# Table numbers read four per register load in a graph attention and relation kernel

## The reference

```python
h = relu(layernorm(x))                                   # layer 0: attention with 8 heads
Q, K, V = h @ Wq, h @ Wk, h @ Wv
score = (Q[dst] * K[src]).sum(-1) / sqrt(32) + relu(edge_attr @ W1 + b1) @ W2 + b2
alpha = softmax of score over the edges of one dst
x = x + segment_sum(alpha * V[src], dst) @ Wo + bo
h = relu(layernorm(x))                                   # layer 1: 16 relations with gates
msg = (h @ W_rel[type])[src] * edge_weight * sigmoid(h @ gate_rel[type])[src]
x = x + relu(segment_sum(msg, dst))
```

## Time and profile before

| | |
|---|---|
| median of 3 runs | 5581.06 us (5578.73 to 5584.89) |
| the profiled execution, its own time | 5578.26 us |
| its span, first to last instruction | 5576.5 us |
| busy over the span | PE 86%, DVE 63%, ACT 59%, POOL 58% |
| mean granted clock of TensorE | 0.878 |

### The profile page before, as it was taken

One profiled execution on the slowest core, in us unless ns is written; L12 is line 12 of the kernel. 1 busy time (PEld: TensorE's weight loads), 2 busy tenths in 40 slices (PEclk: granted clock), 3 DMA queues, 4 the chain that ended last, 5 costly groups with the idle time before them and its releaser, 6 DMA issues. The chain is left out here.

```text
span 5576.5 us, 110596 instructions
## 1 busy us (share of the span) xinstructions
PE 4808.8 (86%) x21476; PEld 2762.5 (50%) x21477; DVE 3500.7 (63%) x8094; ACT 3299.5 (59%) x8030; POOL 3249.0 (58%) x3312
## 2 busy tenths in 40 slices
PE   8899999999999999999799999877777767766666
PEld 5455555555555555555444444444444444444443
DVE  6599999999999999999933333333333333333334
ACT  3588888888888888888644444333333333333333
POOL 0266666666666666666600000177777777777776
PEclk9999999999999999999999999966666676677777
DMA  4577777777777777777644444433333333333335
GB/s 138 165 226 224 228 225 224 228 225 224 228 225 224 228 225 225 228 224 223 181 142 141 142 141 140 135 106 105 106 105 105 105 105 106 105 105 105 105 105 141
DMA packets 551967, 929.49 MB, mean 167 GB/s; under 512 B 112846, under 2 KB 361824, under 8 KB 551905
## 3 DMA queue, kind: packets, MB, share of 16 engines
q0 software_dynamic: 208384, 648.75, 40.9%
q1 hardware_dynamic: 343520, 280.03, 15.7%
HBM read 795.60 MB, written 132.88 MB: 166 GB/s over the span
## 5 line engine op out<-in xcount | busy, mean ns | idle before, releaser
L1006 POOL DMA_INDIRECT kv_rows<-kv_d,idx x1664 | 1716.1, 1031 | 844.2 <-issue 464.2
L1767 PE MATMUL m_sums<-m_rows,m_oh 128*128 x3328 | 1399.8, 570 | 580.8 <-ACT m_rows L1748 507.5
L1704 POOL DMA_INDIRECT m_rows<-msg_d,m_idx x1568 | 1487.3, 949 | 507.3 <-issue 471.5
L1748 ACT ACTIVATE m_rows<-m_rows,m_norm 128x256 f32<-128x256 f32 x1568 | 710.8, 500 | 1268.2 <-DMA m_rows<-msg_d,m_idx 1268.2
L1767 PEld LDWEIGHTS m_sums<-m_rows,m_oh 128*128 128x128 f32 x3328 | 842.8, 277 | 1137.9 <-issue 1013.5
L1790 DVE TENSOR_TENSOR agg<-agg,m_sums 128x256 f32 x832 | 350.5, 421 | 1298.1 <-PE m_sums L1767 1294.3
L1183 PE MATMUL sums<-kv_rows,onehot 128*128 128x264 f32 x3328 | 946.2, 407 | 29.1 <-issue 15.5
L1183 PEld LDWEIGHTS sums<-kv_rows,onehot 128*128 128x128 f32 x3328 | 568.7, 191 | 413.0 <-issue 334.6
L1143 PE MATMUL p_q<-shelf,pickT 128*128 x4992 | 698.1, 275 | 19.7 <-ACT pickT L1049 11.1
L1637 PE MATMUL p_m<-wr,h1T 128*128 128x512 f32 x1568 | 710.5, 596 | 0.0
L1026 ACT ACTIVATE hid<-p_hid,b1s 128x512 f32<-128x512 f32 x784 | 496.3, 684 | 334.2 <-PE p_hid L1122 334.2
(11 more groups left out here) (193 smaller groups left out, 4413.0 us busy)
## 6 DMA issues: line engine op xcount, KB each, us to landing
msg_d<-msg SPq DMA_DIRECT2D x196, 512.0 KB, 2.9
dsts<-dstrow_d SPq DMA_DIRECT2D x208, 256.0 KB
ef_raw<-in_edge_attr_dram SPq DMA_DIRECT2D x195, 256.0 KB
kv_rows<-kv_d,idx POOLq DMA_INDIRECT x1664
m_rows<-msg_d,m_idx POOLq DMA_INDIRECT x1568, 2.8
kv_d<-kvo SPq DMA_DIRECT2D x49, 260.0 KB, 2.1
pens<-pens_d SPq DMA_DIRECT2D x104, 96.2 KB
emlp<-mlp_d SPq DMA_DIRECT2D x104, 64.0 KB
```

What stands on the lines that cost most here:

```text
L1006: pool.indirect_dma_start(rows[:, u, k, :], None, kv_d[:, :], bass.IndirectOffsetOnAxis(idx[:, half, c:c + 1], 0)).then_inc(gathered[u], 16)
L1704: pool.indirect_dma_start(rows[:, u, k, :], None, msg_d[:, :], bass.IndirectOffsetOnAxis(idx[:, u // HALF, c:c + 1], 0)).then_inc(gathered ...
L1748: last = nc.scalar.activation(rows[:, u, k, :], rows[:, u, k, :], ACT.Copy, scale=norm[:, bass.ds(2 * g + k, 1)])
L1767: last = nc.tensor.matmul(sums[u % BANKS][:, 0:D], onehot[:, u % HOTS, k, :], rows[:, bass.ds(slot, 1), k, :].rearrange("p a d -> p (a d)" ...
```

## The change

A constant `LOADS` = 4 and a helper `load_four` are added: one call loads four neighbouring numbers of a row into four registers. The fused stage uses it on TensorE for the block numbers of the next four selects, at u = 0, 4, 8 and 12, and on VectorE for those of the next four adds, at the same u; the second load of a number ahead of a chunk's first add goes. The last stage uses it on TensorE and VectorE once in four steps and on SyncE twice for eight groups, of which it uses the second and the fourth number. A duplicate of `IN_RANGE` and `block_of` is dropped. The first select, and single steps at the start and the end of the last stage on VectorE, still load one number.

```diff
+LOADS = 4
+def load_four(nc, eng, row, s, low, high):
+    _, values = nc.values_load_multi_w_load_instructions(row[:, bass.ds(s, LOADS)], engines=(eng.engine,), min_val=low, max_val=high,
+                                                         skip_runtime_bounds_check_because=IN_RANGE)
+    return values
...
-            def select(s, u):
-                b = block_of(nc, pe, t, s)
+            def select(s, u, b):
...
                     if is_step(s + 1):
-                        select(s + 1, u + 1)
+                        if u % LOADS == 0:
+                            ahead = load_four(nc, pe, t["block"], s + 1, 0, BLOCKS - 1)
+                        select(s + 1, u + 1, ahead[u % LOADS])
...
-            def rescale(s, c):
-                b = block_of(nc, dve, t, s)
+            def rescale(s, c, b):
...
-            def add(s, u, c):
-                b = block_of(nc, dve, t, s)
+            def add(s, u, c, b):
...
                         v = u - LATE - 1
+                        if v % LOADS == 0:
+                            behind = load_four(nc, dve, t["block"], s - LATE - 1, 0, BLOCKS - 1)
                         if v % R == 0:
-                            rescale(s - LATE - 1, 2 * i + v // R)
-                        add(s - LATE - 1, v % SLOTS, 2 * i + v // R)
+                            rescale(s - LATE - 1, 2 * i + v // R, behind[0])
+                        add(s - LATE - 1, v % SLOTS, 2 * i + v // R, behind[v % LOADS])
...
-            def free(g):
-                done = nc.values_load(past[:, bass.ds(g, 1)], engines=(sp.engine,), min_val=1, max_val=STEPS,
-                                      skip_runtime_bounds_check_because=IN_RANGE)
-                hold(sp, summed, done & 1023, freed)
+            def free(done):
+                for last in (1, 3):
+                    hold(sp, summed, done[last] & 1023, freed)
...
-                        for last in range(1, HALF, 2):
-                            free(g + last - RING)
+                        for four in range(0, HALF, LOADS):
+                            free(load_four(nc, sp, past, g + four - RING, 1, STEPS))
...
-                    groups = nc.values_load(t["groups"][:, bass.ds(s, 1)], engines=(pe.engine,), min_val=1, max_val=GROUPS,
-                                            skip_runtime_bounds_check_because=IN_RANGE)
+                    if u % LOADS == 0:
+                        four = load_four(nc, pe, t["groups"], s, 1, GROUPS)
+                    groups = four[u % LOADS]
```

More of the change, by code:

```diff
@@ L777, in block_of @@
                           skip_runtime_bounds_check_because=IN_RANGE)
-IN_RANGE = "counted on the chip: s - BLOCKS < group(s) <= s and below GROUPS, block(s) = s - group(s)"
-def block_of(nc, eng, t, s):
-    return nc.values_load(t["block"][:, bass.ds(s, 1)], engines=(eng.engine,), min_val=0, max_val=BLOCKS - 1,
-                          skip_runtime_bounds_check_because=IN_RANGE)
+def load_four(nc, eng, row, s, low, high):
+    _, values = nc.values_load_multi_w_load_instructions(row[:, bass.ds(s, LOADS)], engines=(eng.engine,), min_val=low, max_val=high,
+                                                         skip_runtime_bounds_check_because=IN_RANGE)
+    return values
 SLOTS = 2 * R
@@ L1214, in body @@
                         add_up(s - LATE - 1, u - LATE - 1)
-            select(0, 0)
+            select(0, 0, block_of(nc, pe, t, 0))
             pe.wait_ge(w_in, WIN)
@@ L1782, in prepare, with add @@
                                         ALU.is_equal).then_inc(onehot_ready, 1)
-            def add(s, u):
-                b = block_of(nc, dve, t, s)
+            def add(s, u, b):
                 dve.wait_ge(summed, s + 1)
@@ L1802, in body @@
                     prepare(i, u)
-                    if not (isinstance(i, int) and i == 0 and u < LAG):
-                        add(RING * i + u - LAG, (u - LAG) % RING)
+                    s = RING * i + u - LAG
+                    if u % LOADS == 0 and not (isinstance(i, int) and s < 0):
+                        four = load_four(nc, dve, t["block"], s, 0, BLOCKS - 1)
+                    if not (isinstance(i, int) and s < 0):
+                        add(s, (u - LAG) % RING, block_of(nc, dve, t, s) if isinstance(i, int) and s < 2 else four[u % LOADS])
             nc.vector.memset(agg[:, :, :], 0.0).then_inc(cleared, 1)
@@ L1813, in _ @@
             for s in range(STEPS - LAG, STEPS):
-                add(s, s % RING)
+                add(s, s % RING, block_of(nc, dve, t, s))
             dve.wait_ge(out_ready, BLOCKS)
```

## The result

The changed kernel takes 5638.48 us, the median of 4 runs (5637.50 to 5639.56); the kernel before took 5580.44 on the same chip (4 runs, 5578.73 to 5584.89). The ratio is 1.0102, with a 95% interval from 1.0089 to 1.0115: slower by 1%, or 58 us. The profiled execution took 5638.3 us, 1.8 more than its span of 5636.5, as before. 5636 was predicted, and slower was given 0.61.

What follows compares the result with a forecast made beforehand. GpSimd was taken to bound the last stage, TensorE and VectorE leading by turns the fused stage. 5578.3 + 59 lost - 4 gained = 5633 us, with 2.8 more for the median 5636; range 5572 to 5675.

Steps and rivals of the forecast that it cites:

- The last stage, at nothing: Last stage: GpSimd's gathers set its time, so longer loads on TensorE, VectorE and SyncE were taken to cost 0.
- The gain at u = 1 and 9: Fused stage, VectorE: a late load ahead of the add goes, giving back 0.04 to 0.05 us twice a body, 4 us.
- TensorE at u = 4 and 12, X - 0.35: Fused stage: load of four ahead of TensorE's select, 0.35 us covered; the rest, X - 0.35, lost twice a body.
- X: Time a load of four takes beyond a load of one: 0.66 us chosen, between 0 and 0.91.
- TensorE at u = 0, X - 0.33: Fused stage, behind the loop's branch: select waits for the load; 0.05 plus 0.28 us covered, X - 0.33 lost once a body.
- VectorE at u = 0 and 8, X - 0.40: Fused stage: load between weigh and add, 0.40 us covered; VectorE leads, so X - 0.40 is lost; counted only at u = 8.
- Of the two delays the longer counts: At u = 0, TensorE's and VectorE's delays meet at the same add, so only the longer, X - 0.33, was counted.
- The sum: A body loses 4X - 1.43, 1.21 us; by 49 bodies 59 us, less 4 us gained.
- The rescale at u = 4 and 12, nothing: Fused stage, VectorE: it follows TensorE there, so dropping the second load and lengthening the first were both put at nothing.
- Rival 1: The four numbers come in one trip, X near 0, so only the 4 us are gained: 5577 us; chance 0.35.

Runs made afterwards that it cites:

- e6: Changed kernel, but TensorE in the fused stage loads two block numbers every second step, from an odd column; 5587.68 us, ratio 1.0001 to the kernel before.
- e9: Changed kernel with the whole block row three columns further right, so TensorE's fused loads start at multiples of four and VectorE's do not; 5605.21 us, ratio 1.0040.
- e5: Changed kernel with the whole block row two columns further right, so no fused load of four starts at a multiple of four; 5671.73 us, ratio 1.0149.
- e8: Changed kernel, but TensorE's fused loads read a second, shifted block row and start at multiples of four; quicker chip, 5580.35 us, ratio 0.9997.
- e2: Same kernel as e8 (TensorE's fused loads from a second, shifted block row), on a slower chip; 6287.00 us, ratio 0.9829.
- e11: Only the last stage as changed, fused stage with single loads on TensorE and VectorE as before; slower chip, 6328.27 us, ratio 0.9870.

## Why the prediction was right, point by point

**The last stage, at nothing:** right in its outcome. Gathers keep 950 ns and 1.25 us, and the longer loads of VectorE there (966 ns) are covered. But SyncE's loads, which the prediction put at up to 0.7 us more, grew by 0.03 (267 to 298 ns), since they start at a multiple of four. That a longer one is covered as well was not tested in any run.

**The gain at u = 1 and 9:** 0.04 to 0.05 predicted, 0.03 measured, twice (650 to 619, 651 to 619).

**TensorE at u = 4 and 12, X - 0.35:** right. TensorE's X is 1002 - 302 = 0.70 us, where 0.66 was chosen; select starts 0.35 us later behind the dot (0.26 to 0.61, medians). VectorE pays 0.38 and 0.40 for it, at the add of u = 5 and 13 and not of u = 6.

**TensorE at u = 0, X - 0.33:** the place right, the size wrong, and the path to it. 0.53 us were lost where 0.37 follows from the real X. I gave the score's room as 0.05, an estimate, and let the delay reach VectorE through `add_up`, with 0.28 more. It reaches it earlier: the scans need the score. The room is 0.17 in all (the changed kernel and e6).

**VectorE at u = 0 and 8, X - 0.40:** the cover right, X wrong. Its load of four starts at a multiple of four, X is 0.04, and nothing is lost; the 0.26 at u = 8 did not occur. That the load itself was mis-sized and not the cover is shown by e9, with 0.27 and 0.24. At u = 8 the changed kernel loses 0.04 through TensorE: its select is late by 0.48 us there (0.26 to 0.74 behind the dot, medians), and 0.04 of it reaches the scan.

**"Of the two delays the longer counts":** wrong. In e5, with both loads long, the 0.55 at the scan and the 0.27 at the add add up, because VectorE's load comes after its scans. With both loads long, as I had assumed, the time would have been near that of e5, 84 us above the kernel before and not 58.

**The sum** holds in part by compensation, and that it comes within 2.5 us of the time is luck. Predicted were 1.21 us lost in a body and 0.08 gained, 1.13; measured are 1.35 lost and 0.14 gained, 1.21. VectorE's term was too large by 0.26 less the 0.04 seen at u = 8, that of u = 0 too small by 0.20 (0.53 for 0.33), TensorE's two by 0.16 (0.78 for 0.62), the gains by 0.06. The count of bodies helped once more: 49 were reckoned with, and the loss stands in the loop's 46, 1.23 us in each (46 x 1.23 = 56.5 us; 49 x 1.13 = 55 were predicted).

**The rescale at u = 4 and 12, nothing:** right on balance. Without its second load the add comes 0.04 us sooner, and VectorE, which follows there, waits that much longer a step on (in e8 by 0.07 and 0.05, with the 0.03 of u = 1 and 9 in it).

**X itself.** The trip of one number less register arithmetic, 221 ns, was the right price of one more number, but only from a column that is no multiple of four (233 on TensorE, 220 on VectorE). Rival 1, one trip for all four, is what the durations of the others look like: in e8 all fused loads are such, and the ratio is 0.9997. The Trainium skill ("Runtime: NRT & Kernel Launch", section "Instruction fetch mechanics") states about 200 ns for each register of a `TENSOR_LOAD`, even in bulk. The loads here from a column that is no multiple of four come near it, with 0.22 to 0.23 us; those from a multiple of four do not, with 0.03 to 0.04 us for three more registers. Neither I nor that rule had asked where the four numbers lie.

## What to carry to other kernels

Before several neighbouring numbers are loaded into registers at once, put the first at a multiple of 16 bytes, if need be by a second, shifted copy of the row. It took the loss away here and gained nothing that could be measured (e8), since the loads of one had been covered. Read such a load's duration by stage and by start column, since a median over both mixes them. And follow a late queue to the first instruction that waits for it on the leading engine, then ask of a second delay whether it lies behind the first (they add) or beside it (the longer counts).

## What the runs showed of the hardware that I had not expected

- A register load of four 32-bit numbers from a multiple of 16 bytes takes 298 ns on SyncE, 332 on TensorE, 344 on VectorE, where one takes 267, 302 and 306. From one, two or three numbers further on it takes 965 on VectorE, from one or three 1002 on TensorE, where two was not tried. Two from an odd column take 534 on TensorE, eight from a multiple of eight 591. Two from an even column were not tried.
- The price follows the column: within 40 ns the same on the queues of TensorE and VectorE, the same in both stages, in partition 0 and in partition 96 (e2, e8), and, by the median, on chips whose whole time differs by 14%.
- Two chips took 6391 and 6407 us for the kernel before, which ran in 5580 to 5587 elsewhere. Its own trace from there is missing; those of the other kernels show waits for a queue of up to 7.3 us, and register arithmetic of 46 ns (median) that takes up to 719 (e11).
